# Fewer, wider comparisons in the adjacency-building stage of a graph network kernel, and running ranks with fewer ones products

## The reference

```python
h = relu(layernorm(x))
# layer 0, a hypergraph convolution applied twice; D, B are the in and out degrees
e   = B_inv * segment_sum((h @ W)[src], dst)      # gather by src, sum by dst
out = D_inv * segment_sum(e[dst], src) + b        # gather by dst, sum by src
x = x + out
# layer 1: messages from edges
h = relu(layernorm(x))
m = silu(silu([h[src], h[dst], w] @ eW1 + eb1) @ eW2 + eb2)
x = x + silu([h, segment_sum(m, src)] @ nW1 + nb1) @ nW2 + nb2
```

## Time and profile before

| | us |
|---|---|
| median of 3 runs | 8857.22 |
| lowest, highest | 8846.52, 8869.20 |
| the profiled execution, its time | 8864.02 |
| its span in the profile | 8862.3 |
| VectorE, TensorE busy, whole span | 7406.3, 7877.5 |
| ScalarE, GpSimd busy, whole span | 5157.5, 2812.5 |

### The profile page before, as it was taken

The page is one execution under the profiler, slowest core; times in us unless marked ns, Lnnn a source line. Parts: engine busy times, 40 slices in busy tenths (PEclk is TensorE's granted clock), DMA queues, the critical chain, the costliest instruction groups (busy, mean ns, idle before and its releaser), DMA issues. The chain is left out here.

```text
span 8862.3 us, 258190 instructions
## 1 busy us (share of the span) xinstructions
PE 7877.5 (89%) x80997; PEld 7191.2 (81%) x80997; DVE 7406.3 (84%) x20481; ACT 5157.5 (58%) x14322; POOL 2812.5 (32%) x4182
## 2 busy tenths in 40 slices
PE   2989998999989988999888899869999999999997
PEld 2777777777777778999788888759998999999995
DVE  7999999999999995777688888548888888888884
ACT  3777777777777770000577788425555555555553
POOL 4977778777777750000000000001111111111110
PEclk9999999999999999999799999759999999999998
DMA  2767667766676677666699999643333333333333
GB/s 71 158 152 157 154 153 157 155 155 153 156 156 153 156 159 199 190 191 170 148 223 222 214 245 245 139 142 109 104 106 106 103 106 106 105 104 105 107 104 74
DMA packets 1523049, 1310.03 MB, mean 148 GB/s; under 512 B 797344, under 2 KB 1337364, under 8 KB 1521212
## 3 DMA queue, kind: packets, MB, share of 16 engines
q1 hardware_dynamic: 1506126, 1269.86, 58.6%
q0 software_dynamic: 14112, 26.84, 1.2%
q10 hardware_dynamic: 1840, 0.53, 0.0%
HBM read 777.89 MB, written 361.62 MB: 129 GB/s over the span
## 5 line engine op out<-in xcount | busy, mean ns | idle before, releaser
L662 POOL TENSOR_SCALAR OH<-iot,kd 128x102 bf16<-128x102 bf16 x3440 | 2285.3, 683 | 3.5 <-PE S L799 3.5
L2257 POOL DMA_INDIRECT Qx<-tab_q,tidx x294 | 320.9, 1091 | 4904.5 <-DVE skt L2291 2584.5
L1478 PE MATMUL wp<-AF,XS 128*128 128x256 f32 x9604 | 1196.3, 283 | 167.6 <-issue 123.4
L841 PE MATMUL HP<-T3a,RB 128*128 128x193 bf16 x9604 | 1209.2, 249 | 124.3 <-ACT RB L965 124.3
L1478 PEld LDWEIGHTS wp<-AF,XS 128*128 128x128 f32 x9604 | 1148.5, 191 | 198.4 <-issue 198.3
L1504 ACT ACTIVATE AF<-RG 128x1536 fp32r<-128x1536 uint8 x686 | 1022.9, 1491 | 332.6 <-PE wp L1478 226.0
L965 ACT ACTIVATE RB<-PS 128x256 int16<-128x256 f32 x2401 | 895.6, 379 | 520.2 <-PE PS L826 479.2
L2278 ACT ACTIVATE Z<-Zb 128x512 f32<-128x512 f32 x882 | 556.1, 630 | 994.3 <-DVE Zb L2335 948.8
L841 PEld LDWEIGHTS HP<-T3a,RB 128*128 128x128 fp8e4 x9604 | 858.8, 98 | 249.1 <-issue 160.8
L926 ACT ACTIVATE LH<-LB,pl 128x64 f32<-128x64 bf16 (+8 forms) x4116 | 1008.4, 330 | 0.0
L2335 DVE TENSOR_TENSOR Zb<-p,eb2s 128x512 f32<-128x512 f32 x882 | 609.3, 691 | 450.1 <-PE p L2228 276.9
(11 more groups left out here) (344 smaller groups left out, 15460.4 us busy)
## 6 DMA issues: line engine op xcount, KB each, us to landing
RG<-adjT SPq DMA_DIRECT2D x1372, 224.0 KB, 6.6
sdb<-bk SPq DMA_DIRECT2D x245, 768.0 KB
adj<-RB SPq DMA_DIRECT2D x343, 448.0 KB, 2.8
adjT<-RT SPq DMA_DIRECT2D x686, 224.0 KB, 3.8
RG<-adj SPq DMA_DIRECT2D x686, 224.0 KB, 4.5
sdb<-bk SPq DMA_DIRECT2D x49, 384.0 KB
WR<-wk SPq DMA_DIRECT2D x882, 9.0 KB
tab_p<-Pst SPq DMA_DIRECT2D x25, 512.0 KB, 3.0
```

Source lines behind the costliest of these rows:

```text
L662: ins = e.tensor_scalar(OH[:, g * GT + k, :], iot1[:, 0:KEYS], kd[:, g * GT + k:g * GT + k + 1], None, ALU.is_equal)
L841: ins = e.matmul(HP[:, h * W3:(h + 1) * W3], lhsT=pair[:, x_, h * P:(h + 1) * P], rhs=T3a[:, 2 * (u - 1) + x_, :], start=False, stop=True, ...
L1478: ins = e.matmul(ps[b][:, 0:256], lhsT=XS[:, n * PB + m, :, :].rearrange("p c f -> p (c f)"), rhs=AF[:, (b + n) % 3, m, :], start=n == 0 a ...
```

## The change

1. `unit`: `OB` and `OA` become one `tensor_tensor` of 512 elements over four blocks (`OA`, four wide, from `iot4` and `SBs`), and the two `OD` of a pair become one of 1024 elements. The odd block's value is 1 and no longer 256.
2. `counts`: the odd block's product goes to columns 256 to 511 of the bank, and is not added to the even block's. `keep` reads all 512 columns, the two halves in turn, and writes bytes.
3. `counted`: the row sums of the two blocks are no longer split; one instruction in place of five.
4. `places`: one `tensor_tensor` compares five tiles (`LB`, as wide as the group's widest). A new function `scaled` on DVE multiplies three tiles by both payloads in one instruction, at the end of the group. ACT scales two tiles in place of three (`AT`).
5. `ranks`: DVE adds the one-hots of tiles 0 and 1, and of 2 and 3, of each group (`plus`, in `SP`), two groups ahead of the rank reductions. PE makes three ones products over 306, 204 and 102 columns. `sorted_` copies less.

```diff
-AT = 3
+AT = 2
@@ ranks on TensorE
-                            past(e, v_rk, v - 1)
+                            e.wait_ge(v_rk, added(v))
...
-                            for k in range(GT - 1):
-                                m = GT - 1 - k
-                                ins = e.matmul(b[:, (k + 1) * KEYS:GT * KEYS], lhsT=ones[:, :], rhs=w[:, k:k + 1, :].to_broadcast([P, m, KEYS]),
-                                               start=False, stop=True, skip_group_check=True)
-                            ins.then_inc(p_r, 1)
+                            tiles = b[:, 0:GT * KEYS].rearrange("p (t k) -> p t k", k=KEYS)
+                            e.matmul(tiles[:, 2:GT, :], lhsT=ones[:, :], rhs=SP[g % 2][:, 0:1, :].to_broadcast([P, GT - 2, KEYS]),
+                                     start=False, stop=True, skip_group_check=True)
+                            e.matmul(tiles[:, 1:GT:2, :], lhsT=ones[:, :], rhs=w[:, 0:GT - 1:2, :],
+                                     start=False, stop=True, skip_group_check=True)
+                            e.matmul(tiles[:, GT - 1, :], lhsT=ones[:, :], rhs=SP[g % 2][:, 1, :],
+                                     start=False, stop=True, skip_group_check=True).then_inc(p_r, 1)
@@ counts on TensorE
-                                even = OA[k % PAIRS][:, 0:n * P].rearrange("p (m y) -> p m y", y=n)[:, :, y]
-                                odd = OB[k % PAIRS][:, y, :]
-                                e.matmul(b[:, 0:256], lhsT=even, rhs=OD[k % PAIRS][:, y, :, 0], start=True, stop=False)
-                                ins = e.matmul(b[:, 0:256], lhsT=odd, rhs=OD[k % PAIRS][:, y, :, 1], start=False, stop=True)
+                                at = OA[k % PAIRS][:, 0:2 * n * P].rearrange("p (m y) -> p m y", y=2 * n)
+                                e.matmul(b[:, 0:256], lhsT=at[:, :, 2 * y], rhs=OD[k % PAIRS][:, y, :, 0], start=True, stop=True)
+                                ins = e.matmul(b[:, 256:512], lhsT=at[:, :, 2 * y + 1], rhs=OD[k % PAIRS][:, y, :, 1],
+                                               start=False, stop=True, skip_group_check=True)
@@ keep on ScalarE
-                            e.activation(RB[n % NSLOT][:, k, :].bitcast(i16), bank(u)[:, 0:256], ACT.Copy,
-                                         accum_out=gs[:, u:u + 1]).then_inc(a_u, 1)
+                            e.activation(RB[n % NSLOT][:, k, :].bitcast(u8).rearrange("p (n x) -> p n x", x=2),
+                                         bank(u)[:, :].rearrange("p (x n) -> p n x", x=2), ACT.Copy, accum_out=gs[:, u:u + 1]).then_inc(a_u, 1)
@@ ranks, plus, places and scaled on VectorE
+                            plus(i, g + 2)
+
+                        def plus(i, g):
+
+                            if g >= NGR:
+                                i, g = i + 1, g - NGR
+                            e.wait_ge(v_oh, i * NGR + (g + 1))
+                            past(e, p_r, i * NGR + (g - 1))
+                            w = OH[:, g * GT:g * GT + 4, :].rearrange("p (y x) k -> p y x k", x=2)
+                            e.tensor_tensor(SP[g % 2][:, :, :], w[:, :, 0, :], w[:, :, 1, :], ALU.add).then_inc(v_rk, 1)
...
-                            for k in range(AT):
-                                t = g * GT + k
-                                w = wide_at(t)
-                                ins = e.tensor_scalar(LB[g % 2][:, k, 0:w], by_rank(g, iot1, iotr, w), float(OWN - 1), rk[:, t:t + 1], ALU.add, ALU.is_equal)
-                            ins.then_inc(v_lb, 1)
-                            for k in range(AT, GT):
...
-                                ins = e.scalar_tensor_tensor(LH[g % 2][:, k, :, 0:w], ranked.unsqueeze(1).to_broadcast([P, 2, w]),
-                                                             rk[:, t:t + 1], pl[:, :, t:t + 1].to_broadcast([P, 2, w]),
-                                                             ALU.is_equal, ALU.mult)
-                            ins.then_inc(v_lh, 1)
+                            t, w = g * GT, wide_at(g * GT + GT - 1)
+                            e.tensor_tensor(LB[g % 2][:, :, 0:w], by_rank(g, GT, w), rk[:, t:t + GT].unsqueeze(2).to_broadcast([P, GT, w]),
+                                            ALU.is_equal).then_inc(v_lb, 1)
+
+                        def scaled(i, g, pl):
+
+                            e.wait_ge(v_lb, i * NGR + (g + 1))
+                            n, t, w = GT - AT, g * GT, wide_at(g * GT + GT - 1)
+                            e.tensor_tensor(LH[g % 2][:, AT:GT, :, 0:w], LB[g % 2][:, AT:GT, 0:w].unsqueeze(2).to_broadcast([P, n, 2, w]),
+                                            pl[:, :, t + AT:t + GT].rearrange("p c t -> p t c").unsqueeze(3).to_broadcast([P, n, 2, w]),
+                                            ALU.mult).then_inc(v_lh, 1)
@@ unit on VectorE
-                                for y in range(2 if u < NU - 1 else 1):
-                                    b = 2 * (u + y - 1) + 1
-                                    e.tensor_scalar(OB[k % PAIRS][:, y, :], iot1[:, 0:P], SBk[:, b:b + 1], 256.0, ALU.is_equal, ALU.mult)
...
+                                e.tensor_tensor(OA[k % PAIRS][:, 0:2 * n * P].rearrange("p (m y) -> p m y", y=2 * n), (iot4 if n == 2 else iot2)[:, 0:P, :],
+                                                SBs[:, b:b + 2 * n].unsqueeze(1).to_broadcast([P, P, 2 * n]), ALU.is_equal)
+                                e.tensor_tensor(OD[k % PAIRS][:, 0:n, :, :], iot2[:, :, :].unsqueeze(1).to_broadcast([P, n, 256, 2]),
+                                                SBd[:, b:b + 2 * n].rearrange("p (y x) -> p y x", x=2).unsqueeze(2).to_broadcast([P, n, 256, 2]),
+                                                ALU.is_equal).then_inc(v_un, 1)
```

More of the change, by code:

```diff
@@ L497, in gnn_kernel @@
                 LH = [sbt(p1, f"LH{n}", [P, GT, 2, P], fp32) for n in range(2)]
-                LB = [sbt(p1, f"LB{n}", [P, AT, P], bf16) for n in range(2)]
+                LB = [sbt(p1, f"LB{n}", [P, GT, P], bf16) for n in range(2)]
                 OHf = [sbt(p1, f"OHf{n}", [P, GT, KEYS], fp32) for n in range(2)]
@@ L511, in gnn_kernel @@
                 OZ = sbt(p1, "OZ", [P, 4, 2 * P], bf16)
-                OA = [sbt(p1, f"OA{n}", [P, 2 * P], bf16) for n in range(PAIRS)]
-                OB = [sbt(p1, f"OB{n}", [P, 2, P], bf16) for n in range(PAIRS)]
+                OA = [sbt(p1, f"OA{n}", [P, 4 * P], bf16) for n in range(PAIRS)]
                 OD = [sbt(p1, f"OD{n}", [P, 2, 256, 2], bf16) for n in range(PAIRS)]
                 iot2 = sbt(p1, "iot2", [P, 256, 2], bf16)
-                SBe = sbt(p1, "SBe", [P, NCH], bf16)
+                iot4 = sbt(p1, "iot4", [P, P, 4], bf16)
+                SBs = sbt(p1, "SBs", [P, BLK], bf16)
                 SBd = sbt(p1, "SBd", [P, BLK], bf16)
@@ L525, in gnn_kernel @@
                 rj = sbt(p1, "rj", [P, KEYS], fp32)
+                SP = [sbt(p1, f"SP{n}", [P, 2, KEYS], bf16) for n in range(2)]
                 cb = [sbt(p1, f"cb{n}", [P, KEYS], bf16) for n in range(2)]
@@ L530, in gnn_kernel @@
                 room = sbt(p1, "room", [P, KEYS], bf16)
-                iotr = sbt(p1, "iotr", [P, P], bf16)
                 iofr = sbt(p1, "iofr", [P, P], fp32)
                 d_ct = sem("c_dct")
-                SBk = sbt(p1, "SBk", [P, 2 * KEYS], fp32)
+                SBk = sbt(p1, "SBk", [P, 4], fp32)
                 Ui = sbt(p1, "Ui", [P, P], bf16)
@@ L592, in wide_at, with added, ranked, used @@
                     return WIDE[t % HT]
-                def by_rank(g, up, down, w):
-                    return up[:, 0:w] if g < HG else down[:, P - w:P]
+                def added(v):
+                    return max(2 * v, 1) if isinstance(v, int) else v * 2
+                def ranked(v):
+                    return v * 2 + 3
+                def used(t):
+                    w, g = wide_at(t), t // GT
+                    a = 0 if g < HG else wide_at(g * GT + GT - 1) - w
+                    return slice(a, a + w)
+                def by_rank(g, n, w):
+                    v = iofo[:, 0:w] if g < HG else iofr[:, P - w:P]
+                    return v.unsqueeze(1).to_broadcast([P, n, w])
                 def ends_of(v):
@@ L798, in buckets @@
                                 w = wide_at(g * GT + k)
-                                ins = e.matmul(slots_to(g, w), lhsT=OHf[g % 2][:, k, :], rhs=LH[g % 2][:, k, :, 0:w],
+                                ins = e.matmul(slots_to(g, w), lhsT=OHf[g % 2][:, k, :], rhs=LH[g % 2][:, k, :, used(g * GT + k)],
                                                start=False, stop=True, skip_group_check=True)
@@ L923, in scaled @@
                                 t = g * GT + k
-                                w = wide_at(t)
+                                w = used(t)
                                 for c in range(2):
-                                    ins = e.activation(LH[g % 2][:, k, c, 0:w], LB[g % 2][:, k, 0:w], ACT.Copy, scale=pl[:, c, t:t + 1])
```

(13 more changed lines are left out.)

39 lines of the change are left out of this document (12 added, 27 removed).

## The result

The changed kernel takes 8460.99 us (median of 4, 8451.88 to 8472.97) beside 8856.67 for the kernel before: a ratio of 0.9553, 95% interval 0.9536 to 0.9571. The direction was right.

A forecast was written before the change was run, and what follows sets the result against it. VectorE was taken as the bound, TensorE next. After the change TensorE's 56.0 us plus 3.2 of waits and issue gave a 59.2 us turn; 48 x 5.4 = 259 us less gave 8598 us, range 8470 to 8740.

The forecast's parts named there:

- The ends of the stage, half filled, I leave alone: Building stage's ends and later stages: no gain counted beyond the 48 turns, as no later stage reads anything of new shape.
- The turn: One chunk's time in the building stage: from 64.56 us to 59.2, 5.4 us less, times 48 turns = 259 us.
- rival A: Building stage: TensorE and ScalarE cut the gain, turn 57.7 to 61.5, whole 8526 to 8708 us; chance 0.62.
- B: Building stage: nearly all of the gain arrives, turn 56 to 57.7, whole 8446 to 8526 us; chance 0.15.
- New waits on VectorE: plus behind each rank reduction, waiting for GpSimd's one-hots: no wait; without GpSimd's lead, up to 3.3 us per late group.
- The row that I preferred: ScalarE's keep over 512 elements: priced by widen at +0.25 us each, 12.3 us a turn.
- The 6.2 us for the third tile: ScalarE's scaling in places: two instructions less per group, 28 a turn at 0.22 us, saving 6.2 us a turn.
- so I leave GpSimd at 50: GpSimd's unedited one-hots: busy time stays at 50 us a turn, with 14 us to spare.
- The alternating read (D): ScalarE's keep reading alternate bank halves: at twice the row's time per element, turn 82, whole 9680 us; chance 0.05.
- the lost pace (E): VectorE's merged OA and OD lose the pace of two elements: turn 73.1, whole 9265 us; chance 0.03.
- F: Building stage: no change, something not seen, such as SP's chain of stores, holds the turn at 64; chance 0.03.

The follow-up runs named there:

- units part: Merged OA and OD, two bank halves, bytes out of ScalarE, one instruction in counted and small copies alone, in the kernel before: 8525.96 us, turn 61.4 us.
- Places: The new places, scaled and AT = 2 alone, in the kernel before: 8599.18 us, turn 63.1 us.
- The ones products alone: plus and the ones products over 612 columns alone, in the kernel before: 8690.11 us, turn 65.9 us.

## Why the prediction was wrong

**The step that failed** is "The ends of the stage, half filled, I leave alone, and no later stage reads anything of new shape". It left 0 for the rest of the kernel, and the edge layer alone became 117 us shorter. Shown as its cause is the place of TensorE's code, 117 instructions earlier, for 44 to 52 us, by runs on other chips; for the rest the cause is open. Without the 117 the time would have been about 8461 + 117 = 8578, inside the range and 20 us from the forecast; without 45 of them 8506, inside it too. `SPACE1` and `SPACE2` stand in the kernel before and suggest that somebody had met this; I read past them. The turn was 0.8 us too long in the forecast as well, some 40 us over 48 turns.

**The turn** was forecast at 59.2 and came to 58.4, a gain of 6.2 us in place of 5.4. That is rival A's range (57.7 to 61.5), not B's: what seems nearly all of the gain arriving is the edge layer. But the way to this number was wrong in its terms:

- *VectorE* was to lose 10.9 us a turn and lost 7.1, from 62.3 to 55.1 by the window 1000 to 2700. The units part gave 7.7 where 10.2 were priced; its new pair takes 0.97 us from start to start (mean of 65 pairs from 1000 us on) and not 0.94, 0.8 us a turn, and where the rest went is open. Places gave 0.9 where 3.2 were priced: the old five instructions took 1.00 us a group in the mean, and not the 1.05 between the two groups read, and the new two 0.46 + 0.47 = 0.93, and not 0.82, which came from an fp32 instruction of the edge layer. In the whole they are longer again, 497 and 560 ns against 464 and 544. `plus` cost 2.1, priced at 2.5.
- *New waits on VectorE* were priced at nothing. In the stretch `plus` did wait for nothing, but at the stage's start it waited 29.6 us for GpSimd's one-hots, in 18 waits of up to 12.0, and the first seam is 6 us later. The wait before `LB`, 5.9 us before, was to be filled by `plus`; it is 17.1, by `TD`.
- *ScalarE* was to have 55.8 us and has 52.6. `keep` grew by 599 - 379 = 220 ns and not by 250, which is 10.8 us a turn and not 12.3; the busy time of the units part grew by 9.0, so 1.8 less again, for a reason that no run shows. The Trainium skill's rate (ScalarE: Activation LUTs, What ACT_TABLE_LOAD costs), 0.833 ns an element, gives 213 ns; the measurement agrees with it. The row that I preferred, `widen`, misled me; it reads another type and another memory than `keep`. The 6.2 us for the third tile were 5.9.
- *TensorE* was to have 56.0 and has 54.9. The ones products alone gave 1.5 us of the 2.4 priced; places gave 1.2 and units 0.3, where nothing was priced; that is 3.0 of the 3.9 us in the table. Of the waits that it was to keep, 2.7 us for ScalarE, it kept 17.6 / (649.6 / 58.4) = 1.6.
- *GpSimd* was to stay at 50.1 and has 57.8: "so I leave GpSimd at 50". I had the rows for its slowing by VectorE and took the slowing to go with the share of time alone. The one-hot went from 686 to 789 ns, and 40 of these 100 ns went when `OD` was split again. GpSimd's wait for its load went, and the waits for GpSimd came. A fuller GpSimd is in no rival.

*The alternating read (D)* and *the lost pace (E)* did not come: `keep` is 599 ns long, `OD` 705 (0.69 forecast) and `OA` 429 (0.42). *F* did not either. The busy shares expected, near 95% on TensorE and ScalarE and 87% on VectorE, were 94, 91 and 95, and GpSimd's 99%.

The version with `diagonal` on VectorE is the fastest that computes the whole: 0.9561 of the kernel before (0.9536 to 0.9586), where the changed kernel, in another set, has 0.9633 (0.9597 to 0.9669).

## What to carry to other kernels

An edit that changes the number of an engine's instructions moves all its later code, and here that alone was worth some 50 us. Read the time of the untouched stages first, and if one of them moved, look for stalls with no releaser in its loop; pad the code to tell the one effect from the other before crediting or blaming the edit. When the fullest engine is relieved, go through every engine's idle time for what it depends on: GpSimd's 14 us a turn were spent as soon as VectorE's instructions grew. Parts that each lose or give little can add up to more than their sum when each removes the other's next bound.

## What the runs showed of the hardware

TensorE's edge loop waited 36 to 39 us at one product, in 22 stalls of up to 2.2 us, when its code lay 117 instructions later, and did not when it lay earlier; the edge layer was 44 to 52 us longer for it in the experiments. On the first chip it was 117 us longer, where the granted clock was lower too, and how much of that is the place is not shown. A `tensor_scalar` of 102 elements on GpSimd, 0.54 us at the stage's start, took 0.69 to 0.80 us in the mean by what VectorE ran beside it. With half the elements it took 0.70, and the shortest of each were 0.53 and 0.41: of the mean some 0.26 and 0.29 us are over the shortest.
